# Two products of the router's list table, made by GpSimd beside VectorE's slot comparisons

## The reference

```
h = layernorm(x) * (1 + ca) + sa
x = x + ga * linear_attention(h)          # 16 heads, chunks of 128, divided by a running denominator
h = layernorm(x) * (1 + cb) + sb
dot = h @ expert_embeddings.T             # 8 experts, the 2 largest of each token are kept
ones = (softmax over the 2 kept > 0)
cap_ones = ones where cumsum(ones, over all tokens) <= 512
index = for each expert its tokens, up to 512
x = x + gb * scatter_add(relu(h[index] @ W1[e]) @ W2[e] * weight)
```

## Time and profile before

| | |
|---|---|
| median of 3 runs | 498.42 us (497.28 to 499.82) |
| the profiled execution | 500.41 us, span 498.7 us, mean granted TensorE clock 0.936 |
| busy share of the span | PE 81%, DVE 64%, POOL 45%, ACT 39% |
| lists of batches 0 to 5 made at | 120.8, 159.4, 198.3, 237.0, 275.6, 315.4 us |
| lists of batches 6 and 7 made at | 346.2, 357.4 us |
| span of the expert phase | from about 359 us to the end |

### The profile page before, as it was taken

How to read it: one execution, slowest core, us unless ns; L and a number is a source line. 1 busy time by engine, 2 the same in 40 slices (tenths; PEclk the granted TensorE clock), 3 DMA queues, 4 the chain that set the end, 5 groups by cost and what they waited for, 6 DMA issues and landing times.

```text
span 498.7 us, 9212 instructions
## 1 busy us (share of the span) xinstructions
PE 404.4 (81%) x3238; PEld 286.4 (57%) x3238; DVE 321.5 (64%) x857; ACT 193.7 (39%) x322; POOL 226.4 (45%) x267
## 2 busy tenths in 40 slices
PE   5785987898898998988989988896149999999640
PEld 0442555575575574565565566675038888888540
DVE  5451674778868868778778768966816666665510
ACT  1245324525525534534443541414114555555100
POOL 2124140352353344235236225234274788888554
PEclk9797999999999999999999999996559999999985
DMA  8201300502600600520430330455175777775443
GB/s 255 56 0 35 101 1 26 153 2 69 180 17 31 206 28 8 183 73 5 153 104 5 121 96 1 134 175 191 45 216 167 182 186 197 176 170 98 48 47 43
DMA packets 40338, 49.68 MB, mean 100 GB/s; under 512 B 5881, under 2 KB 32506, under 8 KB 40306
## 3 DMA queue, kind: packets, MB, share of 16 engines
q1 hardware_dynamic: 33138, 36.55, 23.4%
q0 software_dynamic: 7168, 12.72, 13.2%
HBM read 31.84 MB, written 17.42 MB: 99 GB/s over the span
## 4 chain that ended last, share of the span: by engine, by line
PE 52%; DVE 14%; issue 10%; ACT 9%; POOL 8%; DMA 5%; POOLq 1%; SPq 0%; ACTq 0%; DVEq 0%
PE bank L911 12%; PE bank L938 6%; POOL out L636 5%; PE quad L995 5%; PE bank L1025 4%; PE bank L1051 3%; DMA out<-x,list_back 3%; PE bank L960 3%; ACT xhat L739 2%; PE bank L1092 2%; PE bank L1013 2%; DVE in_slot L1551 2%; PE bank L905 2%; POOL xg L623 2%; DMA x_sb<-x 1%
## 5 line engine op out<-in xcount | busy, mean ns | idle before, releaser
L1417 DVE TENSOR_TENSOR sT<-quad,causal 128x1024 f32<-128x1024 f32 x64 | 75.2, 1217 | 18.0 <-PE quad L995 18.0
L526 POOL TENSOR_TENSOR kcum<-qT,kcum 128x512 f32<-128x512 f32 x16 | 20.4, 1275 | 109.8 <-DVE kcum L1383 109.8
L636 POOL DMA_INDIRECT out<-x,list_back x32 | 53.0, 1657 | 10.9 <-issue 7.7
L1223 PE MATMUL bank<-w_hi,in_hi 128*128 128x256 f32 x128 | 37.2, 291 | 9.0 <-DVE in_lo L1686 6.3
L1025 PE MATMUL bank<-sT,v_pad 128*32 128x128 f32 x1024 | 40.8, 278 | 0.0
L840 ACT ACTIVATE in_hi<-quad 128x512 fp32r<-128x512 f32 x32 | 19.1, 598 | 54.3 <-PE quad L1225 54.3
L995 PE MATMUL quad<-q_bd,kT 32*128 32x256 f32 x512 | 38.4, 409 | 0.0
L1051 PE MATMUL bank<-wog,oT 128*128 128x256 f32 x128 | 33.9, 387 | 4.4 <-DVE oT L1407 4.4
L1686 DVE SCALAR_TENSOR_TENSOR in_lo<-quad,in_hi 128x512 fp32r<-128x512 f32 x32 | 22.1, 692 | 22.6 <-ACT in_hi L840 22.6
L1224 PE MATMUL bank<-w_hi,in_lo 128*128 128x256 f32 x128 | 36.2, 283 | 0.0
L1225 PE MATMUL bank<-w_lo,in_hi 128*128 128x256 f32 x128 | 36.2, 283 | 0.0
(11 more groups left out here) (197 smaller groups left out, 954.9 us busy)
## 6 DMA issues: line engine op xcount, KB each, us to landing
token_rows<-h SPq DMA_DIRECT2D x8, 528.0 KB, 3.1
x_sb<-x SPq DMA_DIRECT2D x8, 512.0 KB, 4.3
out<-x SPq DMA_DIRECT2D x8, 512.0 KB, 5.2
token_rows<-mod_all SPq DMA_DIRECT2D x8, 512.0 KB, 4.2
w_sb<-w1T SPq DMA_DIRECT2D x8, 512.0 KB, 3.8
w_sb<-w2T SPq DMA_DIRECT2D x8, 512.0 KB, 5.1
rden<-rden_rows SPq DMA_DIRECT2D x56, 64.0 KB, 2.3
mod_all<-mod_rows SPq DMA_DIRECT2D x8, 384.0 KB, 5.4
```

The costliest lines, as they stand in the source:

```text
L526: gp.tensor_tensor(qk[:, k, :], qT[b.p][:, k, :], kcum[:, k, :], ALU.mult)\
L636: gp.indirect_dma_start(out=out_rows, out_offset=bass.IndirectOffsetOnAxis(ap=list_back[q][:, t:t + 1], axis=0), in_=y_sb[q][:, t, :], in_ ...
L1223: mm(out, a_hi, b_hi, start=first, stop=False)
L1417: v.tensor_tensor(sT[t % 2][:, 8 * a:8 * (a + 1), :].rearrange("p (r s) i -> p r (s i)", s=2), quad[:, 2 * a:2 * a + 2, :].rearrange("p r ...
```

## The change

VectorE keeps the comparison that fills plane 2 and gives a new semaphore, `part_on`; it goes on with the eight comparisons of `in_slot` at once. GpSimd has a new function `in_lists`: it waits for `part_on`, makes planes 1 and 0 by two products, and adds 4 to `tile_no` (from a new constant tile `four`). TensorE's `route_lists` waits for `in_list_on` as well as `slots_on`. In a step `in_lists(route)` is GpSimd's last call, in the tail it follows the second `norm2_tiles(a)` for batch 6 and `row_h(a)` for batch 7.

```diff
-        SMALL = 18
+        SMALL = 14
+            gp.memset(four[:, :, :], float(TILES))
+            def in_lists(b):
+
+                shape = [P, 2 * TILES, LISTS]
+                gp.wait_ge(S["part_on"], b.n + 1)
+                gp.tensor_tensor(in_list[:, :, 1, :], in_list[:, :, 2, :],
+                                 iota_p[:, 0:1].unsqueeze(2).to_broadcast(shape), ALU.mult)\
+                    .then_inc(S["in_list_on"], 1)
+                gp.tensor_tensor(in_list[:, :, 0, :], in_list[:, :, 2, :],
+                                 tile_no[:, :, :].rearrange("p t j -> p (t j)").unsqueeze(2)
+                                 .to_broadcast(shape), ALU.mult).then_inc(S["in_list_on"], 1)
+                gp.wait_ge(S["in_list_on"], 2 * (b.n + 1))
+                gp.tensor_tensor(tile_no[:, :, :], tile_no[:, :, :], four[:, :, :], ALU.add)\
+                    .then_inc(S["tile_no_on"], 1)
+                gp.wait_ge(S["tile_no_on"], b.n + 1)
@@ GpSimd's step @@
                 if early:
                     norm1(early)
+                if route:
+                    in_lists(route)
@@ GpSimd's tail @@
                 norm2_tiles(a, slice(TILES - 1, TILES), 4 * a.n + 4)
+                in_lists(r)
                 row_h(a, xhat_end)
+                in_lists(a)
@@ TensorE's route_lists @@
                 pe.wait_ge(S["slots_on"], b.n + 1)
+                pe.wait_ge(S["in_list_on"], 2 * (b.n + 1))
@@ VectorE's route_places @@
-                mark(v.tensor_tensor(in_list[:, :, 2, :], iota_list[:, :].unsqueeze(1).to_broadcast(shape),
-                                     list_no, ALU.is_equal))
-                mark(v.tensor_scalar(in_list[:, :, 1, :], in_list[:, :, 2, :], iota_p[:, 0:1], None, ALU.mult),
-                     sync=False)
-                mark(v.tensor_tensor(in_list[:, :, 0, :], in_list[:, :, 2, :],
-                                     tile_no[:, :, :].rearrange("p t j -> p (t j)").unsqueeze(2)
-                                     .to_broadcast(shape), ALU.mult))
-                mark(v.tensor_scalar(tile_no[:, :, :], tile_no[:, :, :], float(TILES), None, ALU.add),
-                     sync=False)
+                v.tensor_tensor(in_list[:, :, 2, :], iota_list[:, :].unsqueeze(1).to_broadcast(shape),
+                                list_no, ALU.is_equal).then_inc(S["part_on"], 1)
```

More of the change, by code:

```diff
@@ L133, in adaln_kernel @@
         tile_no = sb("tile_no", [P, TILES, 2])
+        four = sb("four", [P, TILES, 2])
         spare = sb("spare", [P, 96])
@@ L289, in adaln_kernel @@
             stats2 mean2 rstd2_on xhat_on h2_on rh_mm lg_mm count_mm list_mm h2T_on logits_on top_on topi_on
-            gap_on e2_on small oh_on carry_on sum_on slot_on slots_on lists_on row_on
+            gap_on e2_on small oh_on part_on in_list_on tile_no_on carry_on sum_on slot_on slots_on lists_on row_on
             tok_on list_ld back_ld gT_mm x_hi_on x_lo_on m1_mm in_hi_on in_lo_on aside_on w_hi_on w_lo_on w_ld m2_mm y_on scat
```

## The result

The changed kernel takes 506.83 us (median of 6 runs, 501.70 to 508.53), the kernel before 498.64 us (6 runs, 497.28 to 499.82). The ratio is 1.0151, 95% interval 1.0099 to 1.0203: slower. (A ratio is formed over the single runs, so it needn't be the quotient of the two medians.) The forecast was 504.4 us in a range of 496 to 510. The profiled execution took 507.9 us for a span of 506.2, so 7.5 us more than the profiled execution before (500.41).

A forecast was written before the change was run, and what follows sets the result against it. From the list comparison's end (E) the chain runs through VectorE's `in_slot` and `lists_on` to TensorE's second turn of `xn`. Five steps +6.05, batch 5 −0.1, batch 6 0, batch 7 +0.05: +6.0 on 498.42 gives 504.4 us, range 496 to 510.

The forecast's parts named there:

- The forecast's case: Router lists: products block comparisons, then the moved sum blocks `weighted`, `h` or `carry`; +6.0 us in all, chance 0.60.
- what `chosen` gives back: VectorE's `chosen`, no longer beside the sum: 0.26 off in batch 1 and nearly so in three others, 0.62 in batch 2.
- the middle one: Of `weighted`, `h` and `carry` on VectorE, `h` taken as blocked by the sum: net +1.25 us a step.
- the working's upper end: Attention steps, TensorE's second turn of `xn` at its latest: net +1.7 us, from a range of +0.8 to +1.7 a step.
- The last sentence's clause: Sign of being wrong: GpSimd's products taking another time than 0.73 us.
- The bound of 0: Lower bound for the `in_slot` comparisons on VectorE: not blocked by GpSimd's products at all, 0; upper bound +1.42 us.
- Batches 5 to 7: Last batches: batch 5's stall moves rather than goes, net −0.1 us; batch 6, 0; batch 7, +0.05.
- In turn: Rival: GpSimd's products wait until VectorE's eight comparisons are over; +0.3 us in all, 498.8 us, chance 0.13.
- Nothing collides: Rival: comparisons don't wait and VectorE's three small instructions get past before the sum; −3.6 us, 494.8 us, chance 0.14.
- Behind the big sum: Rival: the last `in_slot` comparisons fall behind GpSimd's sum; +2.8 us a step, +15 in all, 513.4 us, chance 0.13.

The follow-up runs named there:

- held: Changed kernel, with GpSimd's `bo_g` and 128x1024 sum also waiting for `lists_on`: 494.12 us, ratio 0.9943 to the kernel before; repeated, 497.24 us, 0.9946.
- sum_first: Changed kernel, with GpSimd's `bo_g` and sum issued ahead of `in_lists`, where they stood before the change: 497.79 us, ratio 1.0006 to the kernel before.
- lists_first: Changed kernel, with VectorE copying the lists ahead of `weighted`, `h` and `carry`: 500.27 us, ratio 0.9999 to the kernel before.
- before_held: Kernel before, products still on VectorE, with GpSimd's `bo_g` and sum waiting for `lists_on`: 498.21 us, ratio 0.9981; repeated, 497.93 us, 0.9973.
- wait_only: Kernel before, products still on VectorE, with GpSimd waiting for `part_on` at the end of each step: 519.64 us, ratio 1.0451.
- the late kernels: Kernel before and changed kernel, both with the sum waiting for `lists_on`, plus one 128x1 GpSimd addition ahead of first gather: 496.19 us both, ratios 0.9973 and 0.9983.

## Why the prediction was right

- *The mechanism.* The forecast's case came in: the comparisons collide with the products, lists at about E+2.7 (2.66; 2.19 in batch 2), then one of `weighted`, `h` and `carry` waits for the moved sum in each of batches 0 to 5, TensorE idles ahead of its second turn with `lists` as the releaser, `chosen` falls to 0.224 everywhere and the 2.04 us `w` is gone. held and sum_first show that the place of `bo_g` and the sum is the cause, lists_first that most of it acts through `lists_on`.
- *The time.* The stretch grew by 7.21, which on the median gives 498.42 + 7.21 = 505.6 against the 504.4 forecast. The ratios of 1.0151 and 1.0098 make 7.5 us (4.9 to 10.1) and 4.9 us (3.1 to 6.7). Both intervals hold the forecast's 6.0, so its size is judged by the profiles alone.
- *The mis-sized term: what `chosen` gives back.* The forecast took +1.25 a step: the second turn at about E+5.79 instead of E+4.28, so +1.51, less 0.26 for a `chosen` that is no longer blocked. The first part was right: measured +1.70, +1.48, +1.08, +1.47 and +1.73 in batches 0 to 4, 7.46 in all against 7.71. The second part was not: from one turn to the next comparison's end the steps into batches 1 to 4 changed by +0.15, −0.41, −0.03 and −0.05, a gain of 0.34 where 1.40 was taken (0.26 + 0.62 + 0.26 + 0.26; the 0.26 of batch 0 falls ahead of this count). `chosen` did get shorter, but `x` then waited 0.25 for TensorE. before_held shows it without the collision: 0.41 gained in batch 2, nothing in 1, 3 and 4. So the five steps cost 7.12 instead of 6.05.
- *Partly luck: which instruction was blocked.* I had taken the middle one, `h`; it was `weighted` in batches 0, 1, 3 and 4, and `carry` in batch 2. The forecast's own times pointed to `weighted`: they start the sum at E+2.68 and `weighted` at E+2.90. The second turn still came where the middle case had it, since the sum came earlier. `in_lists` took less time: the two products took 0.61 and 0.62, not 0.73 and 0.69, and the sum started at E+2.47 (160.66 − 158.19) instead of E+2.68. So `weighted` ended at E+4.91 instead of E+5.05 to E+5.25, and `lists_on` was 0.80 behind it instead of 0.95: E+5.77 where the working had up to E+6.2 for it. That batch 1's +1.63 looks like the +1.7 of the working's upper end is chance, two errors of 0.4 that cancel. In batch 2 the sum started at E+2.96, so `weighted` lost 0.2 and `carry` was caught; the step cost 0.68 where I took 1.05. The last sentence's clause, that I'd be wrong if the products took another time than 0.73, was too strict.
- *The comparisons.* The rule of the Trainium skill, "SBUF — State Buffer", section "Who interferes with whom", was weighed in the prediction for a form that no row showed. The trace now agrees for it: `in_slot`, one SBUF tensor in bf16, takes 0.66 beside the products instead of 0.25. The bound of 0 falls; the price was +0.45 us on the lists, where +0.5 was taken.
- *Batches 5 to 7.* Forecast −0.1, 0 and +0.05, measured +0.03 up to the first comparison of batch 6 and +0.06 for the last two. In batch 5 the turn of `rden` came 0.41 later, where +0.06 was forecast (316.94 to 317.0), and 0.38 of it was made up again behind it.
- *The rivals.* In turn: GpSimd started product 1 at E+0.08, so no. Nothing collides: no. Behind the big sum: `in_slot` was over at 160.80, 0.14 behind the sum's start, and only one comparison met `bo_g`; the case was near but didn't come. wait_only, in which work of the lists' own chain falls behind the sum, shows what such a case costs: 3.6 to 4.4 a step, not the +2.8 I gave it, and TensorE comes back at a lower clock there.

## What to carry to other kernels

An instruction given to an in-order engine brings its wait along, and everything that the program has behind it there starts at a new time: look first at the largest thing behind the wait, and at which small instructions of the critical engine it now lies beside. If both read SBUF, put the large one where the other engine works on PSUM, with a wait if need be; here one such wait turned +1.0% into −0.5% in the series that ran both. When work goes from VectorE to GpSimd and VectorE's next instructions are of the blocked kind, little is saved: here 0.85 us went and 0.82 came back. And before a gain is taken off a sum, look at what the engine would wait for next: the 0.26 us that `chosen` gave back ended in a wait of 0.25 for TensorE.

## What the runs showed of the hardware that I had not expected

- After 3.4 us of idle TensorE the granted clock was 0.61 over the next 3 us and 0.86 over 4 more (wait_only, 121 to 128 us), where it is 1.00 in the kernel before; by the estimate above that is some 1.7 us of TensorE's work.
- The collision lengthens GpSimd's instruction too, if VectorE holds it up: the 128x1024 sum took 2.54 instead of 2.35 beside VectorE's product at 158.55 in wait_only (and in batches 3 and 5), and a 128x4 copy 1.65 instead of 0.76 beside `w_lo`.
- A 128x256 product on GpSimd that reads one bf16 tensor and one repeated f32 column and writes bf16 took 0.61, against 0.71 for two f32 tensors. The operands differ in more than the type, so no run shows what makes the difference.
- A wait of 2.6 to 2.9 us of TensorE for `x`, some 110 us into the expert phase, is there in five profiles of twelve and absent in seven, with the same instructions in that phase but for the one addition of the late kernels. In the pair that I compared, 0.9 us of lag on GpSimd at 392 us went ahead of it, and in four of the five the copy there took 1.64 or 1.65; in the fifth, the first profile of the changed kernel, it took 0.77. The cause stays open.
